# The second residual and its layer-norm statistics, moved from VectorE to TensorE, ScalarE and GpSimd in seven of eight units

## The reference

```
h   = layernorm(x) * gamma + beta
u,z = split(h @ in_proj)                 # 256 channels each
uc  = silu(causal_conv4(u))
dt, Bm, Cm = split(uc @ x_proj)
delta = softplus(dt @ dt_proj + bias)
state = exp(delta*A) * state + delta*Bm*uc   # a scan over 2048 steps, 256 x 16 states
y   = (state . Cm + uc * D) * silu(z)
a   = y @ out_proj + x                   # the block's own residual
x1  = layernorm(x + a)                   # = layernorm(2x + y @ out_proj)  <- the change
out = layernorm(x1 + moe_top2(x1))
```

## Time and profile before

| | |
|---|---|
| median of three runs | 788.7 us |
| the profiled execution, its own time | 791.61 us |
| its span, first to last instruction | 789.9 us |
| scan stage (first scan to last) | about 52 to 570 us |
| DVE, ACT, POOL, PE busy over the span | 85, 54, 71, 75% |
| mean granted TensorE clock | 0.913 |

### The profile page before, as it was taken

The page is one execution under the profiler, slowest core; times in us unless marked ns, Lnnn a source line. Parts: engine busy times, 40 slices in busy tenths (PEclk is TensorE's granted clock), DMA queues, the critical chain, the costliest instruction groups (busy, mean ns, idle before and its releaser), DMA issues. The chain is left out here.

```text
span 789.9 us, 11864 instructions
## 1 busy us (share of the span) xinstructions
PE 592.4 (75%) x3055; PEld 290.2 (37%) x3071; DVE 670.4 (85%) x1349; ACT 428.5 (54%) x886; POOL 562.2 (71%) x538
## 2 busy tenths in 40 slices
PE   9768788887887888788788674676440999998920
PEld 4322222222322222222222121211130899998910
DVE  4287999999999999999998999999823688887855
ACT  3858586577467476657746554334110565555515
POOL 3345877776899799889879788878865356665634
PEclk9899999999999999999999788878755999999975
DMA  3095476566579568647556654864003677776644
GB/s 93 17 224 133 101 172 154 120 160 161 133 163 258 130 160 191 141 119 186 136 132 152 144 124 104 200 158 109 28 28 102 169 201 215 209 211 176 194 167 169
DMA packets 51169, 117.34 MB, mean 149 GB/s; under 512 B 8816, under 2 KB 25008, under 8 KB 43040
## 3 DMA queue, kind: packets, MB, share of 16 engines
q1 hardware_dynamic: 45344, 107.20, 55.7%
q0 software_dynamic: 4320, 8.99, 3.5%
q10 hardware_dynamic: 1440, 0.40, 0.2%
HBM read 100.21 MB, written 16.35 MB: 148 GB/s over the span
## 5 line engine op out<-in xcount | busy, mean ns | idle before, releaser
L553 POOL TENSOR_TENSOR hc<-hs,Crep 128x1024 f32<-128x1024 f32 x128 | 301.0, 2357 | 96.1 <-DVE hs L1382 85.8
L1382 DVE TENSOR_TENSOR_SCAN hs<-bank,state,flow 128x512 f32<-128x512 f32 x256 | 312.9, 1267 | 17.8 <-ACT bank L1125 11.6
L1125 ACT ACTIVATE bank<-bank,negA 128x512 f32<-128x512 f32 x256 | 164.1, 659 | 186.2 <-PE bank L798 182.6
L798 PE MATMUL bank<-delta,sel 64*128 64x512 f32 x512 | 156.7, 691 | 96.6 <-DVE hs L1382 96.2
L1365 DVE TENSOR_TENSOR flow<-flow,bank 128x2048 f32<-128x2048 f32 x63 | 142.9, 2268 | 0.0
L1266 ACT ACTIVATE flow<-bank,b1T 128x128 f32<-128x128 f32 x284 | 80.8, 369 | 57.1 <-PE bank L988 28.7
L798 PEld LDWEIGHTS bank<-delta,sel 64*128 64x128 f32 x512 | 41.8, 198 | 188.7 <-DVE hs L1382 163.6
L673 POOL DMA_INDIRECT results<-flow,idn x71 | 69.8, 983 | 33.1 <-issue 31.3
L807 PE MATMUL bank<-hc,kc 128*32 128x512 f32 x512 | 73.2, 647 | 7.8 <-POOL hc L553 7.8
L996 PE MATMUL bank<-w_sb,flow 128*128 x568 | 75.5, 276 | 4.5 <-ACT flow L1266 3.3
L988 PE MATMUL bank<-flow 128*128 128x128 f32 x568 | 76.8, 279 | 0.0
(11 more groups left out here) (196 smaller groups left out, 793.3 us busy)
## 6 DMA issues: line engine op xcount, KB each, us to landing
flow<-du_d SPq DMA_DIRECT2D x63, 1024.0 KB
flow<-L_ffn_W SPq DMA_DIRECT2D x71, 256.0 KB
xg<-xs SPq DMA_DIRECT2D x71, 66.0 KB
du_d<-du SPq DMA_DIRECT2D x28, 128.0 KB
xin<-L_attn_x SPq DMA_DIRECT2D x8, 256.0 KB, 3.6
hs<-results SPq DMA_DIRECT2D x8, 256.0 KB, 4.7
out<-hc SPq DMA_DIRECT2D x8, 256.0 KB, 2.0
results<-flow,idn POOLq DMA_INDIRECT x71
```

The lines of the kernel that those rows point to most:

```text
L553: nc.gpsimd.tensor_tensor(hc[:, Q % 2, two, :], hs[:, Q % 2, two, :], Crep[u % 3][:].unsqueeze(1).broadcast_to([P, 2, T]), ALU.mult).then_ ...
L798: ins = nc.tensor.matmul(dbank[2 * odd + i][:], sel[rows, odd, q % 4, :], delta[u % 2][rows, q // 4, :])
L1125: nc.scalar.activation(dbank[G % 4][:], dbank[G % 4][:], ACT.Exp, scale=negA[:, ch:ch + 1]).then_inc(s_ex, 1)
L1382: nc.vector.tensor_tensor_scan(hs[:, Q % 2, j, :], dbank[G % 4][:], flow[Q % 3][:, j, :], state[:, Q // QUADS % 2, Q % QUADS, j:j + 1], AL ...
```

## The change

In units 0 to 6 (hosts 1 to 7) PE adds twice the input itself: after the two products of each 128 tokens comes a third matmul of a matrix `twice` (2 on the diagonal) with `xin`. ACT empties the bank into `res` in four instructions that also give row sums (`residual`, g = 17 and 18). GpSimd makes the negative mean out of them (`back_mean`, slot 8). ACT squares the deviations with row sums again (`deviations`, g = 19 and 20). GpSimd makes variance, scale and shift (`back_spread`, slot 10). `xns` moves from g = 22 to 24, `xnT_evac` from 25 to 27, `xn_T` from 25 to 26, `logits` from 28 to 29, `best_two` from 29 to 30. DVE no longer does the residual and its statistics, except for the last unit. Two entries of `KEPT_BUSY` move with it.

```diff
-KEPT_BUSY = {..., 25: (4, "xn", -1), 27: (6, "xn", -1)}
-DRAINED_BY_DVE = {(w, u) for w in ("out", "logits", "ranks") for u in range(UNITS)} | {("T", 1), ("u0", 1)}
+KEPT_BUSY = {..., 26: (4, "xn", -1), 28: (4, "xn", -1)}
+DRAINED_BY_DVE = {(w, u) for w in ("logits", "ranks") for u in range(UNITS)} | {("out", UNITS - 1)} | {("T", 1), ("u0", 1)}
...
+            def back_mean(u):
+                drained(pool, fill_of(u, "out"))
+                after(pool, s_xn, u)
+                nc.gpsimd.tensor_scalar(cnmean[:], sums[:], -1.0 / D, None, ALU.mult).then_inc(s_nm, 1)
+
+            def back_spread(u):
+                pool.wait_ge(s_sq, u + 1)
+                pool.wait_ge(s_nm, u + 1)
+                nc.gpsimd.tensor_scalar(cveps[:], squares[:], 1.0 / D, 1e-5, ALU.mult, ALU.add).then_inc(s_crs, 2)
+                pool.wait_ge(s_crs, 4 * u + 2)
+                nc.gpsimd.tensor_tensor(crstd[:], cveps[:], minus_half[:], ALU.pow).then_inc(s_crs, 1)
+                pool.wait_ge(s_crs, 4 * u + 3)
+                nc.gpsimd.tensor_tensor(cnmr[:], cnmean[:], crstd[:], ALU.mult).then_inc(s_crs, 1)
...
                     if slot == 8 and j >= 1:
-                        back_rstd(j - 1)
+                        back_mean(j - 1)
+                    if slot == 10 and j >= 1:
+                        back_spread(j - 1)
...
+                    if u < UNITS - 1:
+                        pe.wait_ge(s_tw, 1)
+                        ins = nc.tensor.matmul(mbank[:, P * t:P * t + P], twice[:], xin[u % 4][:, t, :], start=False, stop=True)
...
+            def residual(u, ts):                      # ScalarE
+                if ts[0] == 0:
+                    after(act, s_xn, u)
+                    after(act, s_nm, u)
+                o = filled(u, "out")
+                for t in ts:
+                    ins = nc.scalar.activation(res[:, t, :], o[:, P * t:P * t + P], ACT.Identity, accum_out=sums[:, t:t + 1])
+                if TT - 1 in ts:
+                    ins.then_inc(s_fd, 1)
+
+            def deviations(u, ts):                    # ScalarE
+                if ts[0] == 0:
+                    act.wait_ge(s_nm, u + 1)
+                    after(act, s_crs, 4 * u)
+                for t in ts:
+                    ins = nc.scalar.activation(square[:, t, :], res[:, t, :], ACT.Square, bias=cnmean[:, t:t + 1],
+                                               accum_out=squares[:, t:t + 1])
+                if TT - 1 in ts:
+                    ins.then_inc(s_sq, 1)
...
-                    if g == 22 and j >= 1:
+                    if g in (17, 18) and j >= 1:
+                        residual(j - 1, ((0, 1), (2, 3))[g - 17])
+                    if g in (19, 20) and j >= 1:
+                        deviations(j - 1, ((0, 1), (2, 3))[g - 19])
+                    if g == 24 and j >= 1:
                         xns(j - 1)
-                    if g == 25 and j >= 1:
+                    if g == 27 and j >= 1:
                         xnT_evac(j - 1)
...
-                    if g == 16 and j >= 1:            # VectorE
-                        residual(j - 1)
-                    if g == 17 and j >= 1:
-                        back_stats(j - 1)
```

More of the change, by code:

```diff
@@ L59 @@
 FILLS = fill_order()
-KEPT_BUSY = {3: (4, "dt1", 1), 15: (3, "out", -1), 19: (6, "u1", 2), 23: (3, "z0", 2), 25: (4, "xn", -1), 27: (6, "xn", -1)}
-DRAINED_BY_DVE = {(w, u) for w in ("out", "logits", "ranks") for u in range(UNITS)} | {("T", 1), ("u0", 1)}
+KEPT_BUSY = {3: (4, "dt1", 1), 15: (3, "out", -1), 19: (6, "u1", 2), 23: (3, "z0", 2), 26: (4, "xn", -1), 28: (4, "xn", -1)}
+DRAINED_BY_DVE = {(w, u) for w in ("logits", "ranks") for u in range(UNITS)} | {("out", UNITS - 1)} | {("T", 1), ("u0", 1)}
 def fill_of(u, what):
@@ L168, in mamba_moe @@
         cst = sb("cst", [P, TT, 6])
+        twice = sb("twice", [P, P])
+        sums = sb("sums", [P, TT])
+        squares = sb("squares", [P, TT])
+        square = sb("square", [P, TT, D])
         cmv = sb("cmv", [P, TT, 2])
@@ L301, in mamba_moe @@
         s_cag = sem("ln1_aggr")
+        s_tw = sem("two_on_the_diagonal")
+        s_nm = sem("ln1_minus_mean")
+        s_sq = sem("ln1_squares")
         s_crs = sem("ln1_rstd")
@@ L529, in back_rstd @@
             def back_rstd(u):
-                pool.wait_ge(s_cag, u + 1)
+                pool.wait_ge(s_cag, 1)
                 after(pool, s_xn, u)
                 rsqrt(cveps, crstd, cnmean, cnmr, cmv, 1e-5, s_crs, u)
+            def back_mean(u):
[10 more added lines that the diff above has]
+                nc.gpsimd.tensor_tensor(cnmr[:], cnmean[:], crstd[:], ALU.mult).then_inc(s_crs, 1)
             def relu_plus_exp(u):
@@ L642, in _ @@
             link(nc.gpsimd.memset(fillb[:], 0.0))
+            nc.gpsimd.tensor_tensor(twice[:], ident[:], ident[:], ALU.add).then_inc(s_tw, 1)
             pool.wait_ge(s_w2, 64)
@@ L821, in out_proj @@
                         ins = nc.tensor.matmul(mbank[:, P * t:P * t + P], yg[:, h, P * t:P * t + P], woutT[:, h, :],
-                                               start=(h == 0), stop=(h == 1))
+                                               start=(h == 0), stop=(h == 1 and u == UNITS - 1))
+                    if u < UNITS - 1:
+                        pe.wait_ge(s_tw, 1)
+                        ins = nc.tensor.matmul(mbank[:, P * t:P * t + P], twice[:], xin[u % 4][:, t, :], start=False, stop=True)
                 if TT - 1 in ts:
@@ L898, in host @@
                             proj_z(j + 2, 1)
-                    if g == 25:
+                    if g == 26:
                         xn_T(j - 1)
-                    if g == 28:
+                    if g == 29:
                         logits(j - 1)
                     if early:
-                        if g == 29:
+                        if g == 30:
                             proj_x(j + 2, (0,))
-                        if g == 30:
                             proj_x(j + 2, (1,))
@@ L1402, in back_stats @@
                 after(dve, s_crs, 4 * u)
-                moments(cst, res, cmv, s_cst, s_cag, u)
+                moments(cst, res, cmv, s_cst, s_cag, 0)
             def best_two(u):
@@ L1481, in host @@
                         front_stats(j + 3)
-                    if g == 29 and j >= 1:
+                    if g == 30 and j >= 1:
                         best_two(j - 1)
-                    if g == 30 and j == UNITS - 1:
+                    if g == 31 and j == UNITS - 1:
                         one_hots(j - 1)
```

## The result

Four executions of the changed kernel took 795.07 to 801.34 us, median 797.8; four of the kernel before, beside them, 788.27 to 789.2, median 788.65. The ratio is 1.0112 with an interval of 1.0077 to 1.0146: slower by about 9 us. The forecast was 802.8 in a range of 797 to 809; the median lies at the range's foot, where rival (a) stood (the wait as worked out, the locks kinder). The profiled execution took 796.57 us, its span is 794.7, and its mean granted clock 0.881 against 0.913.

What follows compares the result with a forecast made beforehand. DVE was taken to bound the scan stage. Waits less saved work, +11.8 us, plus +2.3 for `oh` and `taken` gave +14.1 on 788.7: 802.8 us, range 797 to 809.

Steps and rivals of the forecast that it cites:

- rival (a): Wait at `xns` as worked out, but `oh` and `taken` are held less: 797.3 to 800.5 us; chance 0.2.
- the locks: DVE operations with two SBUF operands, `oh` and `taken`, wait until a GpSimd `times_c` in flight ends; net +2.3 us.
- The saving on DVE and the work on ACT: Hosts 1 to 7: DVE loses 1.78 us each, 12.5 in all; ACT gains eight instructions at about 0.35 each.
- Rival (c): ACT's accumulating instructions cost 0.78 us each, delaying the decay of 21 and all behind: 808.8 us; chance 0.12.
- PE's extra matmuls: PE at g = 14 and 16: 0.6 us each, costed at nothing; uncovered, 1.2 us a host.
- The step that decides: `xns` on ACT waits for POOL's late `back_spread`, stalling DVE before s25 and s27: hosts 1 to 5 lose 2.33 us each.
- Rival (b): Scale and shift from POOL reach `xns` in time: 12.8 us faster, 776 us; chance 0.08.
- waits and saved work: Scan stage, hosts 1 to 7: +11.7 for hosts 1 to 5, +0.6 for host 6, -0.5 for host 7; sum +11.8 us.
- the sum for `oh` and `taken`: DVE at g = 0: 1.7 us more in each of hosts 3 to 5, 2.8 less at host 6; +2.3 us.
- the three new ones: Longer waits of `oh` or `taken` for slot 15 in hosts 3, 4 and 5: 1.7 us more each.
- the claim that POOL would be 0.6 earlier: When DVE reaches g = 0 of the next host, 2.33 us later, POOL's slot 15 comes 0.6 us earlier.
- the case with 0.55: Wait at `xns` and holds of `oh` and `taken` both as worked out: 800.5 to 806 us; chance 0.55.

Runs made afterwards that it cites:

- first experiment: Changed kernel with `back_spread` on GpSimd moved from the end of slot 10 to slot 9, ahead of `less_negative`: 779.43 us, ratio 0.9873.
- second experiment: Kernel before, residual and statistics still on DVE, with only the changed kernel's new order of operations: 817.38 us, ratio 1.0335.
- third experiment: Changed kernel with the transpose `xn_T` moved from g = 26 to 28, its followers and keep-busy matmuls moved along: 805.0 us, ratio 1.0192.
- fourth experiment: Changed kernel with `oh` and `taken` issued behind the scan of g = 1 instead of g = 0: 820.25 us, ratio 1.0386.

## Why the prediction held, and where it did not

**The saving on DVE and the work on ACT.** As worked out: DVE was busy 14.1 us less, 2.7 of it in the locks, so 11.4 where 12 were said. (Two of the slices that I called 9 are not: the fourth is a 7, the twenty-second an 8.) ACT's accumulating instructions cost about what I took (0.35): from start to start 0.26 us for a residual tile (273.00 to 273.26) and 0.40 for a square (280.93 to 281.33). The decay of 21 ended 5.5 us after s17, worked out 5.43. Rival (c) is out. PE's extra matmuls stayed hidden.

**The step that decides** was right in place and size. `xns` waited 4.63 (said 4 to 5); the stalls are 1.56 (1.7) and 3.43 (3.5) in host 3, and 2.13 (2.4) in host 6; DVE waited 29.6 us for decays (some 26). Moving `back_spread` alone removed them (first experiment); the order alone made them (second). Rival (b), with 776, did not happen here, and is what the first experiment built: 779.4.

**The size of the two terms.** In the profiled executions the stage grew by 8.95 us and the locks fell by 2.67, so 8.95 + 2.67 = 11.6 are left for waits and saved work, predicted 11.8. Hosts 1 to 5 alone, up to s27 of host 5, give 11.7 apart from the locks, as predicted; the two repeats of the changed kernel give 10.4 and 11.5 for the whole stage, so the agreement to 0.2 is luck, that to 1 or 2 us is not. The term that was mis-sized is the sum for `oh` and `taken`: +2.3 predicted, -2.8 measured (-2.7 with the softplus sum), inside its bounds of -3.2 to +6.9. The wait of 3.04 at host 6 went, as said, but `oh` took 1.94 there instead of 0.20; the three new ones did not come, and those of 0.5 to 0.7 us in hosts 3, 5 and 7 of the kernel before went. 8.95 and not 14.1 is this term to 5.0 of 5.2. The profiled executions as wholes differ by 4.96 only: the stage begins 1.8 us earlier in the one after, and what follows it is 2.4 shorter. Ahead of the stage the change adds one GpSimd instruction (`twice`), behind it nothing; over the twelve profiled executions what follows the stage took 191.4 to 196.8 us, with the kernel before, at 196.2, near the top. The medians differ by 9.15, about as much as the stage.

**What failed in that step** was the claim that POOL would be 0.6 earlier. I followed the late `xns` to ACT and DVE, and not to PE, which is behind it too. There it left 3.62 us of idle time at the transpose; the clock was granted at 0.50 afterwards, the four keep-busy matmuls and the sums behind them took 3.85 us together, and slot 12 waited 1.70 for the sums. Slot 15 so began 1.6 us later than the phase that I had used, 315.11 in host 3, and `oh` at 313.48 slipped in ahead of it, where the two do not meet. The third experiment took that wait away and the locks appeared, at 2.19 to 2.64 us. In a forecast that had PE's wait, rival (a) would have been the likeliest.

**The range and the chances.** Slower was right. The lower end was set to take in rival (a), which had 0.2 and is what came; the case with 0.55 did not. That the median stayed inside, by 0.8 us, is luck: the bounds of one term, 10 us apart, hung on the phase of two instructions of 0.2 us, and the two single repeats, 1.0098 and 1.0117 of the kernel before beside them, would put it at 796.4 and 797.9.

**Of the second experiment** my sum failed in the main by leaving out a gap that the moved work used to fill; of the fourth, by taking one `times_c` as the longest lock.

**Of the Trainium skill** ("SBUF — State Buffer", who interferes with whom) the rule on which DVE instructions are held, those with two SBUF inputs, agrees with every lock seen here: `oh`, `taken` and the softplus sum, while the scans and inflows beside them kept their durations (1.28 and 2.26 to 2.28 us). That one may be held over two GpSimd operations in a row is shown by the 5.22 us, and by 5.01 to 5.32 in three other places. Where the DVE instruction began first, the prediction found the rule and a row apart; what decides it there stays open, as said at the fourth experiment. "ScalarE: Activation LUTs" (rules for kernel authors) would leave such additions on VectorE; the first experiment goes the other way, 0.9873, because DVE was full and ACT was not.

## What to carry to other kernels

When work moves off the full engine, follow the value that it makes to whoever waits for it, through the queue of every engine in between: three instructions of together 1.6 us (290.25 to 291.85), queued behind three large ones, cost more than the 1.8 us a host that the move had freed, and moving them back made the same change a gain. A late value stalls its consumer's queue and everything behind that, on each engine that waits for it: follow it to all of them, the idle TensorE's clock included. A small two-operand VectorE instruction beside a stream of large GpSimd ones should be sought in the trace by its duration: its cost hangs on a microsecond of phase (0.20 us when it began 1.63 ahead of the large one, over 5 when it began 0.48 ahead of two), so try its place again after every change.

## What the runs showed of the hardware

- An ACT instruction that also sums its rows shows as two rows, ACTIVATE (0.28, 0.40) and ACTIVATION_READ_ACCUMULATOR (0.19 to 0.21), which overlap to some 0.1.
- A DVE instruction of 0.20 us with two SBUF operands took 5.22, through two GpSimd multiplications, though it began 0.48 us ahead of the first. In twelve traces, operations of its kind that began 0.19 to 0.63 ahead, inside the DMA issue in front, were held (14 of 14), and those that began 0.69 to 0.94 ahead were not (7 of 7).
- TensorE was granted the lower clock in the 2.8 us behind 3.62 us without work, and work that takes 1.06 elsewhere took 1.94 just after.
